# A graph-attention and expert kernel: the first 2048 nodes are routed beside the last edge groups

## What is computed

```python
xn = layernorm(x)                                    # x: 12500 nodes x 256
h = einsum('ni,hif->hnf', xn, W)                     # 8 heads of 32
ea = leaky_relu(s_src[src] + s_dst[dst], 0.2)        # 212500 edges, sorted by dst
ea = exp(ea - segment_max(ea, dst)[dst]); ea = ea / segment_sum(ea, dst)[dst]
gnn = segment_sum(h[src] * ea, dst)
y = xn + linear_attention(xn, 4 heads)
mix = y + gelu(layernorm(y) @ w_fc1 + b_fc1) @ w_fc2 + b_fc2
x = x + gnn + mix
z = layernorm(x)
probs = softmax(z @ gate_w + gate_b); top 2 of 8 experts, the rest 0
x = x + sum_e probs_e * (gelu(z @ W1[e] + b1[e]) @ W2[e] + b2[e])   # 256 -> 512 -> 256
```

## Time and profile before

| | us |
|---|---|
| median of 3 runs (lowest, highest) | 3248.89 (3241.82, 3249.25) |
| span of the profiled execution | 3246.6 |
| busy PE, DVE, ACT, POOL | 2642.4, 2010.3, 1549.7, 2234.9 |
| edge stage ends (last sum copied) | 2283.9 |
| barrier passed, first gather of sums | 2299.3 |
| first product of an expert tile | 2395.1 |

### The profile page before, as it was taken

How to read it: one execution, slowest core, us unless ns; L and a number is a source line. 1 busy time by engine, 2 the same in 40 slices (tenths; PEclk the granted TensorE clock), 3 DMA queues, 4 the chain that set the end, 5 groups by cost and what they waited for, 6 DMA issues and landing times.

```text
span 3246.6 us, 42100 instructions
## 1 busy us (share of the span) xinstructions
PE 2642.4 (81%) x11512; PEld 2052.3 (63%) x11512; DVE 2010.3 (62%) x5442; ACT 1549.7 (48%) x3382; POOL 2234.9 (69%) x2193
## 2 busy tenths in 40 slices
PE   8657767888888888888888887566359999999998
PEld 6546655666666665666656656344247888778887
DVE  7446557667777676777767766677654555445422
ACT  5325544544555554555455554334234545545444
POOL 0277777777777777777777777776476767676554
PEclk9879988999999999999999998777569999999999
DMA  9797766566666666666566665565766676766663
GB/s 276 242 295 211 199 178 169 162 173 177 164 172 180 172 172 170 174 179 171 163 180 172 173 169 153 160 181 136 253 198 146 151 160 148 162 142 131 131 110 62
DMA packets 397637, 561.15 MB, mean 173 GB/s; under 512 B 71912, under 2 KB 317950, under 8 KB 397225
## 3 DMA queue, kind: packets, MB, share of 16 engines
q0 software_dynamic: 123696, 298.61, 36.3%
q1 hardware_dynamic: 196473, 170.69, 18.1%
q10 hardware_dynamic: 77159, 88.50, 10.4%
HBM read 402.42 MB, written 169.68 MB: 176 GB/s over the span
## 4 chain that ended last, share of the span: by engine, by line
PE 65%; DMA 10%; ACT 8%; POOL 8%; issue 6%; DVE 2%; ACTq 0%; SPq 0%; POOLq 0%; DVEq 0%
PE bank L1314 21%; PE bank L2295 11%; PE bank L2308 10%; DMA rows<-table,srcix 9%; PE bank L1095 7%; POOL rows L1232 6%; PE bank L1084 5%; PE bank L1057 2%; PE bank L865 1%; PE bank L605 1%; PE bank L606 1%; ACT L1354 1%; PE bank L2284 1%; ACT xg L842 1%; PE bank L1296 1%
## 5 line engine op out<-in xcount | busy, mean ns | idle before, releaser
L1232 POOL DMA_INDIRECT rows<-table,srcix x1661 | 1600.3, 963 | 506.4 <-issue 354.2
L1314 PE MATMUL bank<-rows,onehot 128*128 128x272 f32 x3328 | 928.6, 426 | 57.4 <-ACT fout L1370 52.0
L1370 ACT ACTIVATE fout<-bank 128x272 f32<-128x272 f32 x1659 | 638.6, 397 | 574.7 <-PE bank L1314 525.3
L1314 PEld LDWEIGHTS bank<-rows,onehot 128*128 128x128 f32 x3328 | 666.5, 208 | 244.3 <-ACT fout L1370 78.7
L1463 DVE TENSOR_TENSOR rows<-rows,bank 128x1024 f32<-128x1024 f32 x416 | 484.0, 1213 | 173.2 <-ACT rows L1359 172.8
L2386 POOL DMA_INDIRECT out<-x_y,x_dest x203 | 325.0, 1601 | 233.2 <-DMA out<-x_y,x_dest 173.4
L2295 PE MATMUL bank<-x_int,x_w1c 128*128 128x256 f32 (+1 forms) x1696 | 379.7, 378 | 25.5 <-issue 22.2
L2308 PE MATMUL bank<-e_w,x_ht 128*128 x1624 | 370.5, 381 | 9.5 <-issue 7.0
L2295 PEld LDWEIGHTS bank<-x_int,x_w1c 128*128 128x128 f32 x1696 | 316.4, 194 | 77.4 <-issue 35.6
L2334 ACT ACTIVATE x_ht<-bank,x_b1c 128x256 f32<-128x256 f32 (+1 forms) x424 | 173.1, 462 | 394.4 <-PE bank L2295 392.9
L2308 PEld LDWEIGHTS bank<-e_w,x_ht 128*128 128x128 f32 x1624 | 300.2, 190 | 51.3 <-issue 14.8
(11 more groups left out here) (405 smaller groups left out, 3246.3 us busy)
## 6 DMA issues: line engine op xcount, KB each, us to landing
frag<-fout ACTq DMA_DIRECT2D x104, 544.0 KB
rows<-table,srcix POOLq DMA_INDIRECT x1661
x_in<-sorted_d SPq DMA_DIRECT2D x97, 260.0 KB, 3.5
x_b2c<-in_L_ffn_b SPq DMA_DIRECT2D x106, 128.0 KB, 3.5
frag<-in_x ACTq DMA_DIRECT2D x1, 13416.0 KB
table<-hr SPq DMA_DIRECT2D x24, 544.0 KB, 4.0
xs<-in_x SPq DMA_DIRECT2D x24, 512.0 KB, 6.0
xg<-in_x SPq DMA_DIRECT2D x24, 512.0 KB, 6.4
```

What stands on the lines that cost most here:

```text
L1232: p.indirect_dma_start(out=B.rows[b][:, j, :], out_offset=None, in_=B.table[:, :], in_offset=bass.IndirectOffsetOnAxis(ap=B.srcix[:, col:c ...
L1314: pe.matmul(B.banks[2 + c % 3][:, 0:ROW], B.onehot[k % 2][:, j, :], B.rows[k % NR][:, j, :], start=True, stop=True).then_inc(S.sum, 1)
L1370: a.activation(B.fout[k % 2][:, j, :], B.banks[2 + c % 3][:, 0:ROW], ACT.Copy).then_inc(S.ev, 1)
```

## The change

It touches five things.

1. **Merging.** The fragment tensor now has the nodes' rows first and the near rows behind them. There are three whole windows (groups 0 to 95), one of 48 chunks (groups 96 to 98) and one of 80 chunks (groups 99 to 103). The fourth window's steps fall into calls 395 to 402. Ahead of it the four engines other than POOL drain and wait for each other (`freed`), since its buffers lie on those of the MLP. Groups 99 and 103 are not prefetched (`held`). The MLP is squeezed from 91 groups into 90, the whole windows end at call 392, where they ended at 404.
2. **Early gathers.** Ahead of group 102 POOL waits for those drains and for the fourth window's store, and issues the 16 `e_fr` gathers of rounds 0 and 1 (nodes 0 to 2047). The gathers of groups 102 and 103 come behind them.
3. **Early routing.** The 240 steps of rounds 0 and 1 run in calls 404 to 412, in PSUM banks 5 to 7, and ahead of the last merge window: 50 in call 404, 140 in calls 405 to 408, 50 in call 412. Their 32 scatters follow POOL's last edge gather. The constants are made by DVE. POOL's drain for the second barrier stands ahead of the scatters, its wait behind them; then come the gathers for rounds 2 and 3.
4. **Weights.** SP waits in the last merge window for the sum of the last chunk and then issues the 16 weight loads. The final merge store is ACT's.
5. **Pace.** No routing step precedes the first expert tile (350 before). Round 2 is due 2 yields ahead of its first slot, so its 158 steps fall into 26 yields, 6.1 in each, where it was 3 to 3.4.

Buffers are placed anew; copies of the last 128 chunks' index rows (`loc_tail`, `srcix_tail`, …) cost two DMAs and two ACT copies in the node stage.

```diff
+SPLIT = 99
+HELD = (SPLIT, GROUPS - 1)
+FETCH_AT = SPLIT + 3
...
+FIRST_FROM = 4 * (SPLIT + 2)
+def schedule():
...
+    return [(0, 0), (MIX_STEPS, MIX_STEPS), (MLP_END, mlp), (WHOLE_END, parts), (PART_FROM, parts + 1), (PART_END, first),
+            (FIRST_FROM - 1, first), (FIRST_FROM, first + 50), (FIRST_FROM + 4, first + 190), (FIRST_FROM + 7, first + 190),
+            (FIRST_FROM + 8, first + routing)]
...
+def first_fetches(p, S, B):
+    p.wait_ge(S.free, FREE)
+    p.wait_ge(S.a_zero, 32)
+    p.wait_ge(S.mg_out, 16 * (BEFORE + 1))
+    for b in range(2):
+        p.wait_ge(S.far[b], 16 * CB * ((SPLIT + 1 - b) // 2))
+    for r in range(FIRST_ROUNDS):
+        for i in range(R_TILES[r]):
+            fetch_sums(p, S, B, r, i)
 def edges_pool(p, S, B, groups):
     for k in groups:
         b = k % NR
+        if k == FETCH_AT:
+            first_fetches(p, S, B)
...
 def edges_tensor(pe, S, B):
...
     for k in range(GROUPS):
-        more, early = k + 1 < GROUPS, k + 2 < GROUPS
+        more = k + 1 < GROUPS
+        early = more and not held(k + 1)
...
+def expert_weights(sp, S, B):
+    sp.wait_ge(S.sum, CB * GROUPS)
+    for e in range(EXPERTS):
+        sp.dma_start(B.w1[:, e, :, :], B.a["L0_ffn_W1"][e].rearrange("(k p) n -> p k n", p=P)).then_inc(S.x_w1, 16)
+    for e in range(EXPERTS):
+        sp.dma_start(B.w2[:, e * HT:(e + 1) * HT, :], B.a["L0_ffn_W2"][e].rearrange("(k p) n -> p k n", p=P)).then_inc(S.x_w, 16)
...
-    due = [(0, sum(round_steps(r) for r in range(FIRST_ROUNDS + 1)))]
-    due += [(order.index(r) - EARLY * (1 + (r == len(ROUNDS) - 1)), sent[r]) for r in range(FIRST_ROUNDS, len(ROUNDS))]
+    lead = lambda r: 2 if r == FIRST_ROUNDS else EARLY * (1 + (r == len(ROUNDS) - 1))
+    due = [(0, 0)] + [(order.index(r) - lead(r), sent[r]) for r in LATER]
...
     edges_pool(p, S, B, range(GROUPS))
-    barrier(p, S, 2)
-    late(route_pool(p, S, B), experts_pool(p, S, B))
+    reach(p, S)
+    for _ in route_pool(p, S, B, FIRST):
+        pass
+    p.wait_ge(S.stage, MEET[2])
+    later_pool(p, S, B)
+    late(route_pool(p, S, B, LATER), experts_pool(p, S, B))
```

More of the change, by code:

```diff
@@ L1533, in merge_tensor @@
+def merge_tensor(pe, S, B, windows):
     bk = B.banks
-    for w, (b0, m) in enumerate(WINDOWS):
-        last = B.last[w % 2]
+    for w, c0, m, n in numbered(windows):
+        M = B.merges[w]
+        last = M.last[w % 2]
+        if w == BEFORE:
+            yield from freed(pe, S)
         yield from idle(4)
@@ L1928, in steps @@
         yield
-    for r in range(len(ROUNDS)):
+    for r in rounds:
         yield from marked(r, steps(r))
```

516 lines of the change are left out of this document (316 added, 200 removed).

## The result

The change made the kernel **slower**: 3274.86 us, median of four runs (3267.96 to 3281.92), against 3248.76 (3241.82 to 3249.25). The ratio is 1.0088, with a 95% interval of 1.0066 to 1.0111, so +0.9%. The forecast was 3255 with a range of 3228 to 3282, and a chance of 0.33 for slower by over 0.3%.

A forecast was written before the change was run, and what follows sets the result against it. Bounds: POOL's gather issue up to group 101, waits around the barrier, then PE in the expert stage. First product 2392.0 plus 860.4 gives 3252.4; with 2.3 from span to median, 3255 us, range 3228 to 3282.

The forecast's parts named there:

- Part 1, POOL's wait: Edge stage, ahead of group 102: POOL waits 17.7 us (14 to 20) for the fourth window's store, until 2239.4.
- Part 2, sixteen gathers: Ahead of group 102: sixteen gathers at 1.27 us, 1.7 us lengthening in all; group 102's scores at 2283.4, before 2246.4.
- rival C: DVE holds the interface shared with POOL through all eight two-input operations, 9.8 us instead of 1.7: 3263; chance 0.05.
- Part 3, the tail: Group 102's scores to the last sum: 65 us where it was 37.5, last sum at 2348.4.
- lower end: Bound for the tail if all DVE's waits are filled: DVE's bare work, 51.9 us.
- rival A: Faster: routing fits into the waits, tail some 52 us and POOL's wait 15, about 3238; chance 0.28.
- Part 4: Last sum to first expert product: 14.4 MB at 380 GB/s takes 37.9 us; first product at 2392.0, before 2395.1.
- Part 5, the expert stage: First product to the end: eleven rounds instead of ten, 8.9 us more, 860.4 us where it was 851.5.
- The allowance of 0 to 10: Head of the expert stage: possible extra us for adding a round at 6.1 steps a yield, not in the sum.
- rival B: Slower: round 2's scatters are late on POOL, so PE waits for slot 9's rows; 14 us, 3269; chance 0.22.
- D: Slower: POOL's wait ahead of group 102 is held back by engine drains, a store or later sums; +12, 3267; chance 0.06.
- The signs: Forecast wrong if tail 55 us or less, first product waits for scatters, or PE idles over 5 us ahead of slot 9.

The follow-up runs named there:

- e0: The changed kernel run again with no edit; median 3265.0 us, ratio 1.0079 to the kernel before.
- e6: Changed kernel with 110 routing steps in call 404, 20 more by call 412, and 110 after the last sum; ratio 1.0035 to the kernel before.
- e5: Changed kernel with all sixteen weight loads issued behind the barrier, after the pad block and round 2's e_x loads; ratio 1.0109 to the kernel before.
- e7: Kernel before with only rounds 0 and 1 routed ahead of the first slot, round 2 due 2 yields ahead of its own; ratio 1.0096.
- e10: e6 with sums gathered ahead of group 103, 60 routing steps each in calls 408 and 412, the rest after the last sum; ratio 1.0011 to the kernel before.
- e4: Changed kernel with round 3 due 5 yields and round 4 due 8 yields ahead of their first slots; ratio 1.0115 to the kernel before.
- e2: Changed kernel with only the eight W2 loads issued behind the barrier, after the pad block and round 2's e_x; ratio 1.0108 to the kernel before.
- e9: e10 plus the first 26 steps of round 2 ahead of the first slot; ratio 1.0016 to the kernel before.

## Why the prediction was right or wrong

**Part 1, POOL's wait: right.** 16.6 us where 17.7 were forecast (14 to 20).

**Part 2, sixteen gathers: right.** From the first gather of sums to group 102's scores 43.4 us, forecast 44.0. Of the 32 gathers three are clearly lengthened, and one (at 2247.31) by 0.2 us:

```profile
2251.27 1.56 POOL L1930 DMA_INDIRECT e_fr<-frag,nodeix  x1 [0.30 <-issue]
...
2260.65 1.29 POOL L1362 DMA_INDIRECT rows<-table,srcix_tail  x1 [0.31 <-issue]
...
2263.51 1.43 POOL L1362 DMA_INDIRECT rows<-table,srcix_tail  x1 [0.30 <-issue]
```

That is 0.6, 0.3 and 0.5 over the usual 0.95, with the fourth 1.6 us against the 1.7 taken. By DVE's timeline each of the four lies beside one of the four pairs of operations with two inputs. The rule of the Trainium skill ("GPSIMD Engine Reference", section 1, Specifications), which gives no length, names the right pair of engines, and the trace agrees in that. Held for the whole length of eight operations it would be 9.8 us, which the trace refutes, and rival C with it.

**Part 3, the tail: right in its sum and its longest wait, not in its lower end.** 62.3 us against 65 (60.0 in e0), far from the 52 of rival A. PE's transposes and gate products of round 1 were put at 8.3 us of waiting, and the row shows it:

```profile
2308.20 0.23 DVE L2199 TENSOR_TENSOR e_lg<-bank,e_gb 128x64 f32<-128x64 f32 x1 [8.35 <-PE bank L2053]
```

The lower end of 51.9 called DVE's bare work is too high. It counts a round's second half from start to end, 9.9 us, in which DVE is busy for 7.5:

```profile
2348.56:2358.57 10.01, 1.09 (x4) 0.93 (x4) 7.47 (x45) 0.26 (x1) 7.57 (x9) 0.54 1.08 375
```

And it takes all the edge work of the old tail, 28.2 us, of which 23.0 fall in the new one; with 17.6 of routing DVE's work there is 40.6 us. The rest of the 62.3 is waits. The reason given for them, fixed lists in which short operations wait for each other, is borne out by e6, where moving 110 steps out took 21 us off the tail.

**Part 4: right in the sum, by luck.** The gap was 50.0 us and not 43.6. The bytes were as forecast and the rate was not. From the first weight load to PE's first transpose, with the columns of the earlier trace rows:

```profile
2343.90:2388.30 44.40, 3.75 (x13) 2.08 (x13) 12.25 (x37) 1.26 (x6) 21.97 (x23) 0.50 1.06 326
```

That is 14.5 MB at 326 GB/s, where 14.4 MB at 380 were taken. Nor are the weights the last to come: W2's last load lands at 2374.4 and not near 2385. Last come the pad block (landed at 2379.2) and, behind it, the first slot's rows, since SP reaches the barrier only when it has issued the weights, 22 us. The early end of parts 1 to 3 (6.8 us) made up for the 6.4 that were missing; the agreement at the first product to 0.4 us is luck. That an early issue of the weights pays is borne out (e5: 12.5 us later without it).

**Part 5, the expert stage: wrong, and this is the step that failed.** "A round costs 67.69 less 8 x 7.35 = 8.9 us", plus 0 to 10. One more round beside the first slots cost 18.2 us by the profile of after, 20.8 in e0, 20.8 in e7. The 8.9 is what a round costs in the steady stretch, with a round's chain spread over eight slots. In the head PE has 6.5 us more work and 11.7 more without work. In its old place the round had cost nothing (e7: 111.0 us from the last sum to the first product without it, 111.2 with it), so all of its price is new. The allowance of 0 to 10 was the right size and in the wrong place, in the range and not in the sum. On top came 7 us between slots 60 and 105 and 13 behind the last (POOL's output scatters), seen in the first profile and hardly in e0 (0 and 2); the forecast had no term for it.

**The rivals.** B came nearest in number (3269) and to the measured side, but not by its mechanism. Round 2's scatters were late indeed:

```profile
2415.99 1.62 POOL L2583 DMA_INDIRECT out<-x_y,x_dest  x1 [18.92 <-DVE x_y L2564]
...
2442.72 1.60 POOL L1945 DMA_INDIRECT sorted_d<-e_hn,e_row  x1 [0.30 <-issue]
```

They start 51 us behind the first product (2442.72), not 36 or so, and POOL idles 18.92 us ahead of its first output scatter. But PE never waits for a slot's rows in that window; it waits for ACT's rows of rounds 2, 3 and 4. A, C and D were refuted: the tail (A), the lengthened gathers (C), a wait of 16.6 us (D).

**The signs.** Of the signs that the forecast would be wrong, the tail (62.3 us, not 55 or less) and the scatters (landed before the first product could wait for them) did not come. PE did stand idle for over 5 us ahead of slot 9: 5.7 us at 2453.0, for round 3's rows.

**The number.** 3274.9 lies 20 us above the forecast of 3255 and outside the 3245 to 3262 that the forecast alone had. The wide range holds it because it reached up to rival B with a dearer head; B's mechanism did not occur, a dearer head did, and the late chain of POOL, which adds 13 us in the first profile, was in no term.

**Why much moved and the time little.** Against before, e0's profile pays 54 us more up to the last sum, gets 61 back between it and the first product, loses 21 in slots 0 to 20, and some 2 more at the end. The gap behind the barrier is work that has to be done; put beside the edge groups it took nearly as long as by itself, and it had been the cover under which round 2 was routed.

## What to carry to other kernels

Price a piece of work that is moved by the waits of the place where it goes, not by what it costs in a steady stretch where its chain is spread out: a round was 9 us there and 18 to 21 in the head. Ask too what the old idle time was hiding: shortening it took away the place in which another round had been free. When each engine runs a fixed list, a chain that crosses three engines hides best where none of them has other work behind it; e6 and e10 found such places and won back most of the loss. And look at what a long row of issues holds up on its own queue: the barrier, a pad block, the first rows.

## What the runs showed that was not expected

Executions of one changed kernel differ by 6 to 25 us (e4 by 6, e0 by 11, e10 by 22, e2 by 25), where the kernel before stayed within 6 beside e0, 11 beside e10 and 13 beside e9, and in two profiles (after, e4) the last output scatter ends 29 to 30 us behind the last slot's transposes and not 13 to 21 as in the others. POOL's output scatters each wait for the last one's landing; the cause of the upper level stays open. A slot's rows that land in 3.5 us in the steady state take 6.6 us beside gathers of sums (e10) and 10.8 while W2 is still landing (e2).
